# A four-turn expert loop: one turn more between row transposes and second products

## The chip, the cores and the metric

The kernel runs on one core of a Trainium2 chip. The metric is the device time of one execution in microseconds (us), the median of several runs. A core has a tensor engine (PE), a vector engine (DVE), a scalar engine (ACT), GpSimd (POOL) and a sync engine (SP). Each works through a list of its own in program order. They wait for each other by semaphores, and an engine that waits holds up all that stands behind the wait in its list. ACT and SP also issue plain transfers, POOL the indirect ones.

## The reference, cut to what matters

Two layers of cross attention, attention and feed forward run over 2048 tokens of 256 numbers. The last stage, the only one that the change touches, is a mixture of 160 experts with 8 chosen for each token:

```
h1     = silu(einsum('th,eih->eti', x, w_gate))      # first products
h1w    = h1 * combine.T[:, :, None]
routed = einsum('eti,ehi->th', h1w, w_down)          # second products
```

The kernel computes only the chosen pairs of token and expert, 16384 of them.

## The kernel before, in words

An earlier stage has sorted copies of the token rows into pages of 64 rows. All rows of a page have the same expert. There are 416 pages; eight of them are a unit, so there are 52 units, and a unit has two doubles of four pages. The function `experts` (line 938 on) works on them in a Python loop that is unrolled into the engines' lists. Its parts, for unit m:

- `load(m)`, SP: reads eight expert numbers from a table, waits until the second products of unit m-4 are done (`D.wait`, the ring of weights holds four units), and issues eight weight transfers of 256 KB (line 934). A number that is out of bounds makes the transfer skip itself: the page then uses weights that are there already.
- `rows_sp(m)`, SP: issues two of a unit's eight fetches of 64 rows (line 971). On SP the order is load(0), rows_sp(1), load(1), rows_sp(2) and so on, so `rows_sp(m+1)` stands behind `load(m)` and its wait.
- `rows_act(m)`, ACT: the other six fetches. `room_for` makes both wait until the results of unit m-8 are stored.
- `turn(m)`: eight PE transposes of rows (line 1001), then two DVE copies out of PSUM (line 1005).
- `up(m)`: 32 first products on PE (line 1016), which wait for the weights and for the copies of the turn; then one silu on ACT (line 1021).
- `flip(m)`: four PE transposes of the silu's result (line 1028), one DVE copy (line 1032).
- `down(m)`: sixteen second products (line 1042), two DVE copies to `y` (line 1048), and after each of them two indirect scatters by POOL into `y_d` (line 1052).
- `weigh(b)`: small DVE work on the routing weights (lines 1060 to 1073), four pieces in each turn of the loop.

A turn of the loop is, in PE's list, turn(m), down(m-2), flip(m-1), up(m). DVE's list has in one turn: two copies of turn(m), two copies of down(m-2), the copy of flip(m-1), weigh. PE's semaphores are counts: T for turn, U for up, V for flip, D for down. Such a signal is raised by the last matmul of its group.

After the loop a last stage reads all results back and sums eight for each token. It starts when the last scatter has landed.

Of the kernel before, what the change touches and what calls it, by code (L numbers as in the profile page):

```python
# [33 lines left out]
UNITS = DOUBLES // 2  # L34
# [903 lines left out]
def experts(nc, a, sem, bank, ident, table, xs_d, y_d, X, tops, rates, spots, wts, spare, rings, dchain, out):  # L938


    pe, dve, act, pool, sp = nc.tensor, nc.vector, nc.scalar, nc.gpsimd, nc.sync
    FLIP, DOWN, AHEAD, WEIGHED, EARLY = 1, 2, 4, 12, 3
    FETCHED, RESULTS, HELD = 16, 6, 2
    ex, pT, xw, slot_id, w, xgT, (hidden, h), s_rows, s_table, s_w = rings
    ph = ExitStack()
    with ph:
# [41 lines left out]
        def rows_act(m):  # L988
            page = load_numbers(nc, mybir.EngineType.Activation, table[1], m, 8)
            room_for(act, m)  # L990
            for k in range(at_sp(m), 8):
                fetch(act, m, k // 2, k % 2, page[k])

        def turn(m):
            pe.wait_ge(s_g[m % (FETCHED // 2)], (m // (FETCHED // 2) + 1) * 128)
            for d in (2 * m, 2 * m + 1):
                bk = bank[d % 2]
                T.wait(pe, "dve", d - 2)
                for c in range(2):
                    for g in range(2):  # L1000
                        last = pe.transpose(bk[:, (2 * c + g) * P:(2 * c + g + 1) * P], xg[:, d % FETCHED, g, c * P:(c + 1) * P], ident[:, :])  # L1001
                T.done("pe", last)
                T.wait(dve, "pe", d)
                U.wait(dve, "pe", m - HELD)
                T.done("dve", dve.tensor_copy(xgT[d % 4], bk[:, :]))  # L1005

        def up(m):
            bk = bank[2 + m % 2]
            pe.wait_ge(s_w[m % DEEP], (m // DEEP + 1) * 128)
            T.wait(pe, "dve", 2 * m + 1)  # L1010
            U.wait(pe, "act", m - 2)
            for g in range(4):
                for c in range(2):
                    for half in range(2):
                        at = (2 * c + g % 2) * P + half * PAGE
                        last = pe.matmul(bk[half * PAGE:(half + 1) * PAGE, g * P:(g + 1) * P], xgT[(2 * m + g // 2) % 4][:, at:at + PAGE],  # L1016
                                         w[m % DEEP * 8 + 2 * g + half][:, c * P:(c + 1) * P], start=(c == 0), stop=(c == 1))
            U.done("pe", last)
            U.wait(act, "pe", m)
            V.wait(act, "pe", m - HELD)  # L1020
            U.done("act", act.activation(hidden[m % HELD], bk[:, :], ACT.Silu))  # L1021

        def flip(m):
            bk = bank[4 + m % 2]
            U.wait(pe, "act", m)
            V.wait(pe, "dve", m - 2)
            for g in range(4):
                last = pe.transpose(bk[:, g * P:(g + 1) * P], hidden[m % HELD][:, g * P:(g + 1) * P], ident[:, :])  # L1028
            V.done("pe", last)
            V.wait(dve, "pe", m)  # L1030
            D.wait(dve, "pe", 2 * (m - HELD) + 1)
            V.done("dve", dve.tensor_copy(h[m % HELD], bk[:, :]))  # L1032
# [59 lines left out]
        for m in range(UNITS + DOWN):  # L1092
            if m < UNITS:
                turn(m)
            if DOWN <= m:
                down(m - DOWN)
            if FLIP <= m < UNITS + FLIP:
                flip(m - FLIP)
            if m < UNITS:
                up(m)  # L1100
                for n in range(min(2 * m + EARLY, m + AHEAD), min(2 * m + 2 + EARLY, m + 1 + AHEAD, UNITS)):
                    rows_act(n)
                for b in range(4 * m, 4 * m + 4):
                    weigh(b)
# [61 lines left out]
        for k in range(half_k + 1, TOPK):  # L1166
            m = k - half_k
# [643 lines left out]
def program(nc, a, out, plan):  # L1811
    ctx = ExitStack()
    with ctx:
# [7 lines left out]
        def sem(name):  # L1821
# [44 lines left out]
        phase2(nc, a, turns, keys_values, (tops, rates, spots, table, xs_d, xf_d), rings, sem, bank, X, XN, ident, small, dchain, pool_waits, resident,  # L1866
               kT, vv, *prepared[0:3], sc)
        experts(nc, a, sem, bank, ident, table, xs_d, y_d, X, tops, rates, spots, wts, spare, rings, dchain, out)


# [53 lines left out]
```

How the kernel before makes its waits and increments, by code:

```python
    def link(self, ins):  # L99
        self.n += 1
        ins.then_inc(self.sem, 1)
        self.eng.wait_ge(self.sem, self.n)
# [99 lines left out]
    def wait(self, eng, events, i):  # L202
        if i >= 0:
            e, k = max(self.at.get(event, ("pe", 1)) for event in ([events] if isinstance(events, str) else events))
            eng.wait_ge(self.sem[e], i * self.per[e] + k)
# [23 lines left out]
    def keys_values(i, banks_free=None):  # L229
        z = i % 2
        yield
        G.wait(sp, "v3", i - 2)
        sp.dma_start(cT[z][:, :, :], a["ctx2"][i]).then_inc(s_ctx[z], 16)
        yield
        pe.wait_ge(s_ctx[z], (i // 2 + 1) * 16)
        if i == 0:
            banks_free()
        for m in range(2):
# [34 lines left out]
def phase2(nc, a, turns, keys_values, routes, rings, sem, bank, X, XN, ident, small, dchain, pool_waits, resident, kT, vv, qs, qb, bg2, sc):  # L273
# [74 lines left out]
            pool.memset(xw[z][:, :, DIM:WIDE], 0.0).then_inc(s_set, 1)  # L348
        last_row = pool.to_reg(ROWS - 1)
        pe.transpose(bank[6][0:1, 0:P], sc[:, 7:8], ident[:, :]).then_inc(s_max, 1)
        dve.memset(ones_e[:, :], 1.0).then_inc(s_set, 1)
        dve.memset(lift[:, :], -1.0).then_inc(s_set, 1)
        dve.wait_ge(s_max, 1)
        dve.tensor_reduce(sc[0:1, 3:4], bank[6][0:1, 0:P], AX.X, ALU.max).then_inc(s_max, 1)
        pe.wait_ge(s_max, 2)
        pe.matmul(bank[7][:, 0:1], ones[0:1, 0, :], sc[0:1, 3:4], start=True, stop=True).then_inc(s_max, 1)
        dve.wait_ge(s_max, 3)
        link(dve.tensor_copy(sc[:, 2:3], bank[7][:, 0:1]))
```

## Time and profile before

| | us |
|---|---|
| median of 3 runs (1536.27 to 1544.11) | 1537.04 |
| span of the profiled execution | 1537.4 |
| the loop's steady part, 44 units | 365.56 |
| last scatters, 1461.91 to 1485.80 | 23.89 |
| last stage, 1485.80 to 1537.40 | 51.60 |

The profiled execution's span is 0.4 us above the median of the runs; nothing outside the span is reported. A start time in the rows below is counted from the start of the span. In the profile a matmul's end is modelled from its start, while the end of a copy or of a silu is measured.

### The profile page before, as it was taken

Reading aid. Unit: us, or ns where it says so; the run is one execution under the profiler, and the core shown is the slowest. Engines: PE = TensorE matmul, PEld = TensorE weight load, DVE = VectorE, ACT = ScalarE, POOL = GpSimd, SP = SyncE. Lnnn points to the kernel's source line nnn. Section 1 sums busy time; section 2 is a strip of 40 time slices with the busy share of each in tenths; the row PEclk is TensorE's granted clock in tenths of the full one; section 3 lists DMA queues with packets and bytes.
Section 4 is the critical chain, followed back from the end, with each engine's and each line's share of the span. In section 5 each row is a group of like instructions: output and inputs, shape, how many; then the busy total and the mean of one; then the engine's idle time right before and its main releaser. Section 6 shows DMA issues by size and latency. Waiting matters only on the chain. (4 is left out here: it accounts for less than half of the span.)

```text
span 1537.4 us, 34403 instructions
## 1 busy us (share of the span) xinstructions
PE 1310.5 (85%) x11693; PEld 947.1 (62%) x11693; DVE 934.3 (61%) x2676; ACT 595.3 (39%) x1709; POOL 549.3 (36%) x717
## 2 busy tenths in 40 slices
PE   5999999999986899999999998755777877787747
PEld 3676767667653676776667776634555555565525
DVE  2576667666654478777887777553544545454437
ACT  2455545454532666675666566310000000000031
POOL 0010111101001136666656564631445444454440
PEclk8999999999995899999999999987999999989968
DMA  9223424233220002111111211339565666665549
GB/s 305 85 72 120 142 75 144 96 121 120 73 95 28 15 23 68 62 51 60 67 58 52 77 35 41 96 108 291 149 180 165 165 192 180 188 186 172 152 159 366
DMA packets 124879, 185.73 MB, mean 121 GB/s; under 512 B 23286, under 2 KB 90517, under 8 KB 122785
## 3 DMA queue, kind: packets, MB, share of 16 engines
q1 hardware_dynamic: 53776, 91.55, 19.0%
q10 hardware_dynamic: 54800, 57.31, 12.4%
q0 software_dynamic: 16128, 34.67, 6.3%
q8 instruction: 95, 1.56, 0.4%
q14 instruction: 80, 0.65, 0.1%
HBM read 190.88 MB, written 78.25 MB: 175 GB/s over the span
## 5 line engine op out<-in xcount | busy, mean ns | idle before, releaser
L1052 POOL DMA_INDIRECT y_d<-y,xg x208 | 206.4, 992 | 258.9 <-DVE y L1048 211.1
L1005 DVE COPY ex<-bank 128x512 f32<-128x512 f32 x104 | 67.1, 686 | 230.1 <-issue 112.9
L1021 ACT ACTIVATE ex<-bank 128x512 f32<-128x512 f32 x52 | 31.0, 597 | 418.9 <-remote 224.8
L773 POOL DMA_INDIRECT xs_d<-xw,slot_id x128 | 135.0, 1055 | 29.8 <-issue 27.9
L472 ACT ACTIVATE ex<-bank,nmC 128x256 f32<-128x256 f32 x256 | 119.1, 483 | 13.1 <-DVE nmC L466 12.8
L485 PE MATMUL bank<-ident,ex 128*128 128x128 f32 x512 | 81.5, 290 | 19.1 <-ACT ex L472 16.9
L485 PEld LDWEIGHTS bank<-ident,ex 128*128 128x128 f32 x512 | 63.8, 149 | 54.1 <-ACT ex L472 21.3
L466 DVE TENSOR_REDUCE nmC<-bank 128x2 f32<-128x512 f32 x128 | 82.9, 682 | 5.7 <-PE bank L457 4.8
L1028 PE MATMUL bank<-ident,ex 128*128 128x128 f32 x208 | 35.8, 297 | 54.0 <-ACT ex L1021 52.1
L1311 POOL TENSOR_TENSOR stB<-stB,small 128x1 f32<-128x1 f32 x32 | 20.2, 632 | 165.3 <-DVE stB L1308 165.3
L1465 ACT ACTIVATE sm<-sm,nm 128x256 f32<-128x256 f32 x128 | 63.4, 499 | 36.0 <-DVE nm L1457 35.8
L491 ACT COPY pTC<-bank 128x512 f32<-128x512 f32 x112 | 64.9, 594 | 26.2 <-PE bank L485 19.1
L1685 POOL COPY recxB<-recB 128x128 f32<-128x128 f32 x32 | 8.4, 291 | 184.9 <-DVE recB L1680 184.9
L1028 PEld LDWEIGHTS bank<-ident,ex 128*128 128x128 f32 x208 | 22.7, 145 | 81.9 <-ACT ex L1021 78.6
L1048 DVE COPY y<-bank 128x512 f32<-128x512 f32 x104 | 66.9, 681 | 10.0 <-PE bank L1042 8.4
L1001 PE MATMUL bank<-ident,xg 128*128 128x128 f32 x416 | 61.0, 293 | 8.5 <-DMA xg<-xs_d 8.5
L1338 PE MATMUL bank<-cT,wk0a 128*128 128x512 f32 x128 | 63.8, 623 | 3.6 <-DVE nm L1457 3.6
L457 PE MATMUL bank<-kTC,qxC 32*128 32x256 f32 x512 | 61.1, 438 | 6.1 <-ACT ex L472 3.3
L1001 PEld LDWEIGHTS bank<-ident,xg 128*128 128x128 f32 x416 | 48.5, 150 | 19.5 <-issue 10.5
L1369 PE MATMUL bank<-pTA,ctxA 128*128 128x512 f32 x128 | 59.1, 605 | 0.7 <-DVE pTA L1485 0.4
L505 POOL TENSOR_TENSOR recx<-recC,half 128x128 f32<-128x128 f32 x64 | 24.1, 406 | 95.6 <-DVE recC L499 95.6
L472 ACT ACTIVATION_READ_ACCUMULATOR ex<-bank,nmC 128x1 f32 x256 | 54.8, 214 | 0.0
(390 smaller groups left out, 3418.2 us busy)
## 6 DMA issues: line engine op xcount, KB each, us to landing
xs_d<-zeros ACTq DMA_DIRECT2D x16, 1768.0 KB, 7.3
pTC<-in_wexp SPq DMA_DIRECT2D x104, 256.0 KB
xg<-xs_d ACTq DMA_DIRECT2D x306, 68.0 KB
cT<-in_ctx SPq DMA_DIRECT2D x32, 512.0 KB, 4.0
wh<-in_wexp SPq DMA_DIRECT2D x52, 256.0 KB
cT<-in_wexp SPq DMA_DIRECT2D x52, 256.0 KB
kTC<-in_wexp SPq DMA_DIRECT2D x52, 256.0 KB
vvC<-in_wexp SPq DMA_DIRECT2D x52, 256.0 KB
```

Source lines behind the costliest of these rows:

```text
L457: last = pe.matmul(bank[hp][:, 256 * b:256 * b + 256], qx[z][rows, m, b, :, :].rearrange("p h t -> p (h t)"), kT[z][rows, m, 256 * b:256 * ...
L466: D.done(i, "dve", dve.tensor_reduce(nm[:, u, :], bank[hp][:, :].rearrange("p (b n) -> p b n", b=2), AX.X, ALU.max, negate=True), f"m{u}")
L472: last = act.activation(ex[:, u, 256 * b:256 * b + 256], bank[hp][:, 256 * b:256 * b + 256], ACT.Exp, bias=nm[:, u, b:b + 1], accum_out=su ...
L485: last = pe.transpose(bk[:, q * P:(q + 1) * P], ex[:, u, q * P:(q + 1) * P], ident[:, :])
L491: D.done(i, en, copy(pT[:, u, :], bk[:, :]), f"pT{u}e")
L773: pool.indirect_dma_start(out=xs_d, out_offset=bass.IndirectOffsetOnAxis(ap=slot_id[z][:, k:k + 1], axis=0), in_=xw[z][:, k, :], in_offset ...
L1001: last = pe.transpose(bk[:, (2 * c + g) * P:(2 * c + g + 1) * P], xg[:, d % FETCHED, g, c * P:(c + 1) * P], ident[:, :])
L1005: T.done("dve", dve.tensor_copy(xgT[d % 4], bk[:, :]))
L1048: D.done("dve", dve.tensor_copy(y[:, n, :, :].rearrange("p g n -> p (g n)"), bk[:, :]))
L1052: pool.indirect_dma_start(out=y_d, out_offset=bass.IndirectOffsetOnAxis(ap=who, axis=0), in_=y[:, n, g, :], in_offset=None, bounds_check=l ...
L1338: pe.matmul(bank[m][:, :], wka[:, m * P:(m + 1) * P], cT[z][:, 0, :], start=True, stop=False)
L1465: last = act.activation(sm[:, j, n, :], sm[:, j, n, :], ACT.Exp, bias=nm[:, h:h + 1], scale=-1.0, accum_out=sums[:, h:h + 1])
```

## The change

The loop gets one more turn of depth. In turn m PE now does turn(m), up(m-1), flip(m-2), down(m-3); before it was turn(m), down(m-2), flip(m-1), up(m). The silu and the DVE copies move with their matmuls: DVE's list becomes two copies of turn(m), the copy of flip(m-2), two copies of down(m-3), weigh. The loop runs 55 turns and not 54. `rows_act` is called for unit m+3 and not m+4 in turn m. Since the silu in that turn is now that of unit m-1, the fetches of a unit keep their place behind the same silu. SP's list does not change, only the moment at which its waits on D are met. Rings, PSUM banks and the number of instructions stay as they are.

```diff
-    FLIP, DOWN, AHEAD, WEIGHED, EARLY = 1, 2, 4, 12, 3
+    UP, FLIP, DOWN, AHEAD, WEIGHED, EARLY = 1, 2, 3, 3, 12, 3
...
         for m in range(UNITS + DOWN):
             if m < UNITS:
                 turn(m)
+            if UP <= m < UNITS + UP:
+                up(m - UP)
+            if FLIP <= m < UNITS + FLIP:
+                flip(m - FLIP)
             if DOWN <= m:
                 down(m - DOWN)
-            if FLIP <= m < UNITS + FLIP:
-                flip(m - FLIP)
             if m < UNITS:
-                up(m)
                 for n in range(min(2 * m + EARLY, m + AHEAD), min(2 * m + 2 + EARLY, m + 1 + AHEAD, UNITS)):
                     rows_act(n)
```

## Rows read from the trace of the kernel before

**Rows 1.** Busy time by stage: loop's start, steady loop, last scatters, last stage
```profile
core 0: us, PE busy (x) PEld busy (x) DVE busy (x) ACT busy (x) POOL busy (x), PEclk, DMA share, GB/s
1033.00:1096.35 63.35, 38.80 (x365) 29.41 (x367) 23.92 (x63) 3.58 (x6) 15.87 (x16) 0.82 0.81 231
1096.35:1461.91 365.56, 288.26 (x2641) 211.55 (x2639) 177.68 (x465) 26.27 (x44) 174.83 (x176) 0.91 0.61 175
1461.91:1485.80 23.89, 14.26 (x122) 9.69 (x118) 7.55 (x12) 1.19 (x2) 15.66 (x16) 0.71 0.15 54
1485.80:1537.40 51.60, 29.75 (x100) 23.26 (x100) 34.18 (x85) 15.98 (x53) 0.00 (x0) 0.74 0.91 366
```
**Rows 2.** Timeline of PE, one period of the steady loop
```profile
1210.82 0.66 PE L1028 MATMUL bank<-ident,ex 128*128 128x128 f32 x4
1211.68 1.97 PE L1016 MATMUL bank<-pTC,ex 128*64 128x128 f32 x32 [0.20 <-issue]
1213.58 1.09 PE L1001 MATMUL bank<-ident,xg 128*128 128x128 f32 x8
1214.60 0.43 PE L1042 MATMUL bank<-kTC,ex 128*64 128x256 f32 x1
...
1217.02 0.42 PE L1042 MATMUL bank<-xw,ex 128*64 128x256 f32 x1 [0.36 <-issue]
1219.18 1.11 PE L1028 MATMUL bank<-ident,ex 128*128 128x128 f32 x4 [1.74 <-ACT ex L1021]
```
**Rows 3.** Timelines of ACT, POOL and DVE, the same period
```profile
1210.17 0.60 ACT L1021 ACTIVATE ex<-bank 128x512 f32<-128x512 f32 x1 [8.05 <-DMA y_d<-y,xg]
1218.53 0.60 ACT L1021 ACTIVATE ex<-bank 128x512 f32<-128x512 f32 x1 [7.76 <-remote]
...
1212.45 0.98 POOL L1052 DMA_INDIRECT y_d<-y,xg  x1 [3.71 <-DVE y L1048]
...
1216.30 0.98 POOL L1052 DMA_INDIRECT y_d<-y,xg  x1 [0.30 <-issue]
1220.75 0.98 POOL L1052 DMA_INDIRECT y_d<-y,xg  x1 [3.47 <-DVE y L1048]
...
1210.29 1.29 DVE L1005 COPY ex<-bank 128x512 f32<-128x512 f32 x2 [4.23 <-issue]
1211.49 1.28 DVE L1048 COPY y<-bank 128x512 f32<-128x512 f32 x2
1212.69 0.68 DVE L1032 COPY ex<-bank 128x512 f32<-128x512 f32 x1
1218.59 1.29 DVE L1005 COPY ex<-bank 128x512 f32<-128x512 f32 x2 [5.22 <-remote]
```
**Rows 4.** Timelines of PE, ACT and POOL: before the second group of scatters, and near the end
```profile
1066.92 1.27 PE L1016 MATMUL bank<-kTC,ex 128*64 128x128 f32 x9
...
1068.24 0.60 ACT L1021 ACTIVATE ex<-bank 128x512 f32<-128x512 f32 x1 [9.69 <-PE bank L1016]
...
1463.47 1.13 PE L1016 MATMUL bank<-kTC,ex 128*64 128x128 f32 x8
...
1464.64 0.60 ACT L1021 ACTIVATE ex<-bank 128x512 f32<-128x512 f32 x1 [5.75 <-PE bank L1016]
...
1461.91 0.98 POOL L1052 DMA_INDIRECT y_d<-y,xg  x1 [3.27 <-DVE y L1048]
...
1483.61 0.98 POOL L1052 DMA_INDIRECT y_d<-y,xg  x1 [0.30 <-issue]
```
**Rows 5.** Timeline of SP's transfers: first without scatters, then in rows 2's period
```profile
1065.04 2.98 SPq L934 DMA_DIRECT2D pTC<-in_wexp  x8
1068.53 1.13 SPq L971 DMA_DIRECT2D xg<-xs_d  x2
...
1211.88 1.21 SPq L971 DMA_DIRECT2D xg<-xs_d  x2
1213.82 0.26 SPq L934 DMA_DIRECT2D wf<-in_wexp  x1
1214.11 4.29 SPq L934 DMA_DIRECT2D cT<-in_wexp  x4
1218.52 0.61 SPq L934 DMA_DIRECT2D kTC<-in_wexp  x3
```
**Rows 6.** Chain of work through one unit's last scatter
```profile
1232.67 0.30 issue
1232.98 2.11 DMA y_d<-y,xg
```
**Rows 7.** DMA queues over 42 units: packets, MB, share of 16 engines
```profile
q1 hardware_dynamic: 19934, 29.94, 29.0%
```
**Rows 8.** Who waited for whom over the same 42 units: us, times, longest
```profile
PE bank L1028 <- ACT ex L1021: 48.4, 34, 2.6
```
**Rows 9.** Timeline of POOL, the loop's first scatter
```profile
1057.55 0.98 POOL L1052 DMA_INDIRECT y_d<-y,xg  x1 [38.24 <-DVE y L1048]
```

## The prediction

> **What bounds the kernel now.** I read the stretches by stage first [rows 1]. The loop's steady part has 176 scatters, so 44 units in 365.56 us: 8.31 us for a unit. PE is marked busy for 79% of it, POOL for 48%, DVE for 49%, and the DMA engines for 61%. No engine is full, so a loop of waits sets the period. I then laid the timelines of one period side by side to find it [rows 2, 3].
>
> PE's first products end at 1213.65 by their rows [rows 2], yet the silu that waits for nothing else starts at 1218.53 [rows 3], 4.9 us later. The transposes that follow them end at 1214.67, and their DVE copies start at 1218.59. So several PE signals of different ages arrive together. I call this moment the release. The preceding one is at 1210.17. PE being behind with its work does not explain it: thirty-two first products and the transposes behind them, which alone take 1.09 us [rows 2], can't end within 0.1 us of each other. Before the second group of scatters the first products end at 1068.19 and the silu starts at 1068.24. Near the loop's end, when SP issues no more weights, they end at 1464.60 and the silu starts at 1464.64, though POOL is scattering [rows 4].
>
> What stands beside the silent stretch is POOL's group of four scatters: it runs from 1212.45 to 1217.28, and the release follows 1.25 us behind [rows 3]. SP suffers in the same stretch: without scatters it issues eight weight transfers in 2.98 us; in the stretch four take 4.29 us [rows 5]. The first matmul group whose signal is lost ends 1.2 us after POOL's start (1213.65), and SP's slow stretch begins 1.66 us after it (1214.11). I read a closed loop: release, two copies of turn, the first copy of down, POOL's start, four scatters, release. In numbers [rows 3]: 1210.17 to 1212.45 is 2.28; POOL 4.83; then 1.25. That is 8.36 against the 8.31 of the mean. PE isn't on it: it needs some 5.5 us after the release and then stands still. This is the reading on which all below rests. It is inferred from times, and I know no cause for it.
>
> **What the change does to that loop.** No instruction is added or removed; the number of copies, scatters and transfers is the same. Four things move.
>
> First, the wait of flip for its silu goes. It cost PE 48.4 us in 42 units, 1.15 us each [rows 8]. PE isn't on the loop, so I count nothing; it is the cover for the half-speed stretches of PE (mean granted clock 0.91 [rows 1]). If PE were the bound it would be worth about 1.15 us a unit (a rival below).
>
> Second, DVE's order. Today three copies stand between release and POOL: two of turn, one of down. They start 0.60 us apart (1211.49 less 1210.29 is two of them [rows 3]). In the new list, turn(m) is the first thing PE does after a release, not the last before one. Its signals should be back before the silence, and its copies done while POOL scatters. The copy of flip now stands before that of down. Flip's matmuls come after the first products, some 3.9 us after the release, so their signal is caught in the silence. That leaves two copies between release and POOL: 2.28 − 0.60 = 1.68. The period is 1.68 + 4.83 + 1.25 = 7.76 us.
>
> Third, what may spoil it: the turn's rows arrive later. Load(m) waits for down(m-4). That used to come at the end of turn m-2, and now comes at the end of turn m-1, and rows_sp(m+1) stands behind it in SP's list while turn(m+1) needs it one period later. The slack was a period more. Count from a release: the queue moved 29.94 MB in 42 units [rows 7], of which 84 row fetches of 68 KB are 5.85, so 92 real weight transfers, 2.2 a unit. A skipped one takes 0.61 / 3 = 0.20 us of SP; the eight of 2.98 us, 0.37 each, I take as the price of a unit with more real ones than the mean [rows 5]. Eight of a mean unit then lie between 1.6 and 3.0 us, and I take 2.6. Add 0.3 for the wait and the first step, 0.5 for the table read between 1068.02 and 1068.53, and 1.13 for two fetches [rows 5]: 4.5 us if nothing disturbs. But the silence begins at 1.68 + 1.66 = 3.3 us. The weights fit, the table and the two fetches fall into it, at 4.29 / 4 = 1.07 us for a step or more; I let them end with it, at about 7.1 to 7.8. The landing isn't shown for them. Its nearest row is a scatter's, 2.11 us [rows 6]; below it I bound it by 0. So rows are there 7.1 to 9.9 us after the release, that is between 0.7 us before the next release and 2.1 us after it. The turn's second signal is raised about 1.4 us later (1.09 and 0.3), at 0.7 to 3.5 us of the next period. The silence takes signals from 1.68 + 1.2 = 2.9 us on. So most turns pass, the late ones are caught. A caught turn puts its two copies back in front of POOL: 2.28 + 0.60 = 2.88, a period of 8.96. If one turn in six is caught the mean is 7.76 + 0.2 = 7.96; that share is an estimate from where 2.9 lies between 0.7 and 3.5, reduced because most units have few real weights and a long period gives SP 1.2 us back. Bounds: none caught, 7.76; half caught, 8.36.
>
> Fourth, depth. The first scatter waits for one turn more, while the first turns are set by the arrival of weights and rows, as before. Every scatter is then a turn late at the start: +8.0 (7.8 at the new period, 8.3 at the old). At the end, from the 49th group's first scatter to the last scatter is 1483.61 + 0.98 − 1461.91 = 22.7 us [rows 4]; there the groups follow each other almost at once, and I count no change. The last stage of 51.60 [rows 1] keeps its work.
>
> **The Trainium skill against the rows.** The rows show SP's plain transfers at 1.07 us each beside POOL's scatters, and at 0.37 without them [rows 5]. The Trainium skill, page "DMA: Bandwidth & Descriptors", section "SWDGE vs HWDGE vs iDMA", says that GpSimd writes its descriptors into rings in SBUF by software and that transfers issued by SP or ACT never use that path. By that rule SP's fetches would be out 4.5 us after the release, no turn would be caught, and the sum would be that of 7.76. The trace does not agree: something is shared.
>
> A second rule gives a rival. In the rows the silu starts 4.9 us after the modelled end of the matmuls [rows 2, 3]. The Trainium skill, page "Perfetto Trace Analysis", section "Tensor Engine Instruction (MATMUL, LD_WEIGHTS)", says that PE's end in a profile is an estimate, and that the signal is sent when PSUM has acknowledged all bytes. By that a late signal would mean late matmuls, and PE would be the bound; the silu and the turn's copy 0.06 us apart speak against it.
>
> **The sum.** From the fourth group of scatters to the 49th there are 45 periods. 45 × (7.96 − 8.31) = −15.8, and +8.0 for depth: −7.8. Against the profiled span: 1537.4 − 7.8 = 1529.6. The span stands 0.4 above the median of the runs, so I say 1529.2. With the bounds of the period: 7.76 gives 1537.4 − 24.8 + 8 = 1520.6; 8.16, a third caught, gives 1538.7.
>
> **Rivals.** *The silence is thinner.* With SP waiting more for D, PE's signals may come back early, as in rows 4, or PE is truly the bound and wins the 1.15 us of its wait. Then the period is 8.31 − 1.15 = 7.16: 45 × −1.15 + 8 = −44, 1494. For it: the prompt silu of rows 4 [rows 4], and PE's late signals if they were late matmuls. Against: the bunch of signals [rows 3]. The skill's second rule above, if it held here, would be this rival. A milder form, flip's signal also ahead of the silence, gives 1.08 + 4.83 + 1.25 = 7.16 as well. Chance 0.15 for 1515 and less.
>
> *Turns are caught in half of the periods.* Mean 8.36: the copies that left the loop come back, and only depth is left: +2.3 + 8 = +10, 1548. For it: signals of the turn due at up to 3.5 us against 2.9. Against: 2.2 real weights a unit leave the mean unit earlier. Chance 0.25 for 1539 to 1552.
>
> *Slower by SP's chain.* If the wait for down(m-4), eight weights and two fetches together end later than 2.9 − 1.4 = 1.5 us after the next release, every turn, PE starts each turn late, second products slide past the release and POOL starts a further 0.5 us or more late: a period of 8.86 and above, 45 × 0.55 + 8 = +33, 1570. It decides when the landing takes over 2.5 us. For it: up(m) too has its weights only one period after load(m) may start. Against: they are issued in 2.6 us, ahead of the silence. Chance 0.15 for over 1552.
>
> The forecast keeps 0.45, for 1515 to 1539.
>
> **Numbers.** About 0.5% (7.7 us) is what a measurement of this kernel can tell from no change: below 1529.3 is faster, above 1544.7 slower. Of the forecast's 0.45, 0.27 lie below 1529.3. Faster is 0.27 + 0.15 = 0.42. Of the 0.25 for half caught 0.10 lie below 1544.7, so the same is 0.18 + 0.10 = 0.28; slower is 0.15 + 0.15 = 0.30. The range that leaves out 2 in 10 is 1507 to 1558; the forecast's own is 1515 to 1539.
>
> **What would show it.** In the profile after: POOL's groups 7.8 to 8.0 us apart; from silu's start to POOL's first scatter about 1.7 us; copies of line 1005 in POOL's shadow and not just behind the silu; SP's two fetches of line 971 between 3 and 8 us after the silu; PE without a wait for ACT on line 1028; the first scatter some 8 to 14 us later than 1057.55 [rows 9]. The prediction is wrong if four copies stand ahead of POOL in most periods, if POOL's groups come closer than 7.5 us, or if PE waits for rows or weights by more than 1 us a turn.

## The result, and the profile after

The changed kernel takes 1552.18 us (4 runs, 1550.0 to 1554.29), the kernel before on the same chip 1537.67 (4 runs). The ratio is 1.0101, 95% interval 1.0078 to 1.0124: slower by 1.0%, 14.5 us. The forecast was 1529.2, faster. The profiled execution has a span of 1553.0 us against 1537.4 before.

First the busy time by stage, cut as in [rows 1]: loop's start, steady loop from the fourth group of scatters to the 49th, last scatters, last stage.

```profile
core 0: us, PE busy (x) PEld busy (x) DVE busy (x) ACT busy (x) POOL busy (x), PEclk, DMA share, GB/s
1033.00:1103.99 70.99, 46.41 (x392) 35.59 (x392) 28.21 (x75) 4.18 (x7) 15.75 (x17) 0.79 0.74 209
1103.99:1476.82 372.83, 278.06 (x2646) 208.16 (x2648) 188.03 (x456) 26.30 (x44) 173.21 (x176) 0.93 0.59 171
1476.82:1500.00 23.18, 8.54 (x86) 5.71 (x82) 5.93 (x9) 0.60 (x1) 15.68 (x16) 0.78 0.16 55
1500.00:1553.00 53.00, 29.03 (x100) 22.79 (x100) 34.18 (x85) 15.99 (x53) 0.00 (x0) 0.77 0.88 357
```

The steady 44 units take 372.83 us, 8.47 each, where they took 8.31. PE is busy for less of it. The moments come from POOL's timeline: first scatter, fourth group, 49th group, last scatter.

```profile
1069.64 0.99 POOL L1052 DMA_INDIRECT y_d<-y,xg  x1 [49.67 <-DVE y L1048]
...
1095.14 0.98 POOL L1052 DMA_INDIRECT y_d<-y,xg  x1 [2.87 <-DVE y L1048]
...
1476.82 0.98 POOL L1052 DMA_INDIRECT y_d<-y,xg  x1 [4.11 <-DVE y L1048]
...
1497.60 0.98 POOL L1052 DMA_INDIRECT y_d<-y,xg  x1 [0.30 <-issue]
```

The first scatter is 12.1 us later than in [rows 9], the fourth group 7.0 us (1088.18 before). The 45 periods between take 381.68 us, 8.48 each; before 8.305. That is +8.0 us. The rest gives +0.7: the tail is 0.9 shorter, the work behind the last scatter 1.6 longer. 7.0 + 8.0 + 0.7 = 15.6, which is the difference of the spans.

Now who waited for whom on PE in the steady loop (total us, times, longest), against [rows 8]:

```profile
PE bank L1001 <- DMA xg<-xs_d: 70.9, 38, 3.6
PE bank L1042 <- issue: 17.3, 37, 1.1
```

Flip's wait for ACT is gone, as the change intended. In its place the transposes wait for their rows, 70.9 us in all, 1.6 us a unit. Two periods show how; SP and PE first, then POOL, ACT and DVE. (The transposes at 1226.49 are of rows that were there in time.)

```profile
1226.68 0.08 SPq L934 DMA_DIRECT2D wf<-in_wexp  x1
1226.94 2.70 SPq L934 DMA_DIRECT2D cT<-in_wexp  x4
1231.07 1.66 SPq L934 DMA_DIRECT2D kTC<-in_wexp  x3
1233.35 1.14 SPq L971 DMA_DIRECT2D xg<-xs_d  x2
...
1226.49 1.09 PE L1001 MATMUL bank<-ident,xg 128*128 128x128 f32 x8
...
1236.34 1.09 PE L1001 MATMUL bank<-ident,xg 128*128 128x128 f32 x8 [2.29 <-DMA xg<-xs_d]
...
1241.47 1.95 PE L1042 MATMUL bank<-pTC,ex 128*64 128x256 f32 x16
```

```profile
1226.65 0.98 POOL L1052 DMA_INDIRECT y_d<-y,xg  x1 [5.16 <-DVE y L1048]
...
1230.56 0.98 POOL L1052 DMA_INDIRECT y_d<-y,xg  x1 [0.30 <-issue]
1234.39 0.98 POOL L1052 DMA_INDIRECT y_d<-y,xg  x1 [2.85 <-DVE y L1048]
...
1243.57 0.98 POOL L1052 DMA_INDIRECT y_d<-y,xg  x1 [4.34 <-DVE y L1048]
...
1232.76 0.60 ACT L1021 ACTIVATE ex<-bank 128x512 f32<-128x512 f32 x1 [8.08 <-remote]
...
1228.89 1.29 DVE L1005 COPY ex<-bank 128x512 f32<-128x512 f32 x2
1232.82 0.69 DVE L1032 COPY ex<-bank 128x512 f32<-128x512 f32 x1 [2.64 <-remote]
```

A group of second products ends at about 1226.5. SP, which waited for it, issues eight weights until 1232.7 and two fetches of rows from 1233.35 to 1234.49. The transposes that need them start at 1236.34, 9.8 us behind the second products. First products, flip and second products follow in PE's list and end at 1243.4. That end is what SP waits for next but one: from one second product to that of two turns later it is 16.9 us, two periods of 8.45. This is a closed chain: neither the transposes nor SP's next weights can come earlier than it allows.

The first period shown, 1226.65 to 1234.39, is 7.74 us, the next 9.18. Of the 45, 24 are under 8.1 us and have a mean of 7.78, the other 21 have 9.29. In the short ones the loop runs as forecast: POOL ends at 1231.54, the silu starts 1.22 us later, and POOL starts 1.63 us behind the silu, with the copies of the turn (1228.89) in its shadow. Over all 24 the median from the silu to POOL's start is 1.70 us.

The profile shows one thing more. SP itself waits little for the second products:

```profile
SPq L934 <- PE bank L1042: 11.3, 12, 2.1
```

Between these waits its list takes 8.26 us a unit (mean over units 5 to 46, reading of the tables included), of a period of 8.5. In the kernel before it takes 8.30 us of 8.33 on this chip and is idle ahead of one load in 42. There no engine waited for it, since the rows arrived 8.1 us ahead of their transposes (mean); now PE waits for what comes out of this full list. So the chain through the second products and SP's list by itself are nearly of one length here, and this chip's profile can't part them.

### The profile page after: what moved, and what is told of

It reads as the page before. It is cut to its first block and busy times, and to the rows that moved or that the text cites. A ratio compares the mean times of both kernels' runs of the same rounds, so it can differ in the third digit from the quotient of the medians.

```text
span 1553.0 us, 34403 instructions
## 1 busy us (share of the span) xinstructions
PE 1303.3 (84%) x11693; PEld 947.4 (61%) x11693; DVE 946.3 (61%) x2676; ACT 595.8 (38%) x1709; POOL 548.4 (35%) x717
## 5 line engine op out<-in xcount | busy, mean ns | idle before, releaser
L1001 PE MATMUL bank<-ident,xg 128*128 128x128 f32 x416 | 66.6, 311 | 104.5 <-DMA xg<-xs_d 98.6
L1001 PEld LDWEIGHTS bank<-ident,xg 128*128 128x128 f32 x416 | 51.7, 156 | 127.3 <-DMA xg<-xs_d 119.3
L1032 DVE COPY ex<-bank 128x512 f32<-128x512 f32 x52 | 36.0, 692 | 150.8 <-PE bank L1028 103.3
L1005 DVE COPY ex<-bank 128x512 f32<-128x512 f32 x104 | 68.2, 687 | 68.2 <-issue 36.9
L485 PE MATMUL bank<-ident,ex 128*128 128x128 f32 x512 | 82.1, 292 | 19.4 <-ACT ex L472 17.5
L485 PEld LDWEIGHTS bank<-ident,ex 128*128 128x128 f32 x512 | 64.3, 150 | 54.2 <-ACT ex L472 22.0
L1048 DVE COPY y<-bank 128x512 f32<-128x512 f32 x104 | 71.4, 690 | 17.8 <-PE bank L1042 14.3
L457 PEld LDWEIGHTS bank<-kTC,qxC 32*128 32x128 f32 x512 | 36.3, 203 | 26.0 <-ACT ex L472 13.4
```

The source lines that it names most:

```text
L457: last = pe.matmul(bank[hp][:, 256 * b:256 * b + 256], qx[z][rows, m, b, :, :].rearrange("p h t -> p (h t)"), kT[z][rows, m, 256 * b:256 * ...
L485: last = pe.transpose(bk[:, q * P:(q + 1) * P], ex[:, u, q * P:(q + 1) * P], ident[:, :])
L1048: D.done("dve", dve.tensor_copy(y[:, n, :, :].rearrange("p g n -> p (g n)"), bk[:, :]))
```

## The experiments

They ran on five chips, each ratio against the kernel before on the same chip. The first chip has no number in the record, so that of e13 and e14, where the kernel before takes 1536.10, may be the same one. Each run is the kernel before or the changed one but for the edit shown.

### The change on other chips

No edit. e5 and e12 are the changed kernel, e6 the kernel before for its trace.

> The changed kernel itself, on whatever chip this call gets. In the first set the kernel before took 1379 and not 1537 us, with no late PE signals; the period there was 5.5 us. Theory A (SP's chain from down(m-4) through eight loads and two fetches to turn(m+1), two periods long): without late signals the chain is about 0.2 + 4.6 + 1.5 + 2 = 8.3 us to turn(m+1) plus 4.9 us from turn to the signal of down, 13.2 / 2 = 6.6 us a period, 1537's counterpart plus 50 us: 1425 to 1440 us where the kernel before takes 1379, PE waiting for rows. Theory C (the loss is depth alone): plus 6 to 9 us, 1386 to 1390. On a chip like the first, A: 1552, C: 1545.

> The kernel before itself, for its trace on this chip. If the late PE signals belong to the chip and not to the kernel, the silu starts either 0.3 us (period 5.4 to 5.6) or 4.6 us (period 8.3) behind the first products in nearly all units, and the same holds for e5.

> The changed kernel itself once more, as the measure for the other three on their chip. If the kernel before takes about 1379 there: 1475 to 1500, period 7.3 to 7.7, ratio 1.07 to 1.085 as before. If it takes about 1537: 1548 to 1556, ratio 1.008 to 1.012, period 8.4 to 8.5.

The kernel before takes 1378.78 us on the chip of e5 and e6, 1379.92 on that of e12: 10% less than on the first chip. The changed kernel takes 1486.53 (ratio 1.0776, 1.0730 to 1.0822) and 1486.21 (1.0786, 1.0751 to 1.0821). My 6.6 us for e5 was too short; it has 7.55 us a period, e12 7.38. What differs for the kernel before is seen in e6's timeline of ACT:

```profile
1204.59 0.60 ACT L1021 ACTIVATE ex<-bank 128x512 f32<-128x512 f32 x1 [4.64 <-PE bank L1016]
1209.95 0.60 ACT L1021 ACTIVATE ex<-bank 128x512 f32<-128x512 f32 x1 [4.76 <-PE bank L1016]
```

Silus are 5.4 us apart. Over all units the silu starts 0.38 us (median) after the start of the last first product, on the first chip 4.61 us. The late signals on which the prediction rests are all but absent here (over 1 us in 5 of 52 units, in 49 on the first chip), and PE sets the period. Busy time from the fourth to the 49th group, e6:

```profile
1056.80:1304.10 247.30, 244.40 (x2706) 184.10 (x2704) 189.20 (x470) 26.88 (x45) 178.60 (x181) 0.99 0.90 262
```

PE is busy for 99% of it. In the changed kernel the same chain is in the open. SP's and PE's timeline in e12, behind it the sums of PE's waits for rows and of SP's for second products, and the busy time of the 45 periods:

```profile
1178.31 0.08 SPq L934 DMA_DIRECT2D wf<-in_wexp  x1
1178.58 1.86 SPq L934 DMA_DIRECT2D cT<-in_wexp  x4
1180.62 0.61 SPq L934 DMA_DIRECT2D kTC<-in_wexp  x3
1181.86 1.14 SPq L971 DMA_DIRECT2D xg<-xs_d  x2
...
1187.25 1.09 PE L1001 MATMUL bank<-ident,xg 128*128 128x128 f32 x8 [3.73 <-DMA xg<-xs_d]
```

```profile
PE bank L1001 <- DMA xg<-xs_d: 70.8, 26, 6.8
...
SPq L934 <- PE bank L1042: 90.5, 31, 8.2
...
1070.90:1403.20 332.30, 261.40 (x2706) 198.70 (x2708) 193.33 (x470) 26.88 (x45) 176.96 (x180) 0.93 0.67 194
```

Here SP's list takes 5.34 us of the period of 7.4, so it is not full, and both waits of the chain can be seen. Against e6 the 45 periods are 85.0 us longer. PE idles for 68.0 of these. The other 17.0 are the same matmuls running longer: after the waits PE's granted clock is in part at the lower level, 0.93 in the mean where e6 has 0.99.

Taken over units 5 to 46, the chain's parts are (means, us):

| | first chip, after | e12 |
|---|---|---|
| second products to SP's first weight | 0.6 | 0.3 |
| eight weights | 5.6 | 2.5 |
| to the first fetch | 0.8 | 0.8 |
| first fetch to the rows' arrival | 2.9 | 4.4 |
| arrival to the transposes | 0.3 | 1.0 |
| transposes to the end of second products | 6.9 | 5.9 |
| sum, two turns | 17.0 | 14.9 |

17.0 / 2 = 8.5 and 14.9 / 2 = 7.4. That these are the measured periods proves nothing by itself, since the parts lie end to end from one unit's second products to those of two units later. What shows the chain at work is how little slack its two waits leave: SP starts 0.6 and 0.3 us behind the second products, where it lagged by 3.6 in the kernel before on the first chip, and the transposes start 0.3 and 1.0 us behind their rows' arrival, where it was 8.1 us. And it shows in what follows when the chain is cut, below. On the first chip that stands against 8.3 us which the late signals took already; elsewhere against PE's 5.4. So the same chain costs 1% there and 8% here.

### Taking the chain apart

e7 and e8 (and again e15, e16): changed kernel and kernel before without weight transfers from unit 4 on, and so without SP's wait for D; the first and second products use the weights of the first four units.

```diff
-            load(m)
+            if m < DEEP:
+                load(m)
...
-            pe.wait_ge(s_w[m % DEEP], (m // DEEP + 1) * 128)
+            pe.wait_ge(s_w[m % DEEP], 128)
```

> The changed kernel with only the first four units' weights loaded and no wait for down(m-4) on SP: units 4 to 51 use what lies in the ring. Theory A: SP no longer hangs on second products, no wait for rows or weights, PE's work sets the period, 5.2 to 5.4 us on a chip without late signals; level with e8 but for depth, within 8 us of it, and 20 us or more below the kernel before. Theory B (the order itself): the loss against e8 stays at over 2%.

> The kernel before with the same weights left out. Theory A: weights land in time before, so only the waits near the loop's start go: 0 to 20 us faster than the kernel before, period as before. If transfers of weights were what slowed the rest (bandwidth), the period would fall clearly.

> The changed kernel without weight transfers and without SP's wait for them from unit 4 on, a second time, in the hope of a chip on which the kernel before takes 1537 (late PE signals); it took 1384 where before took 1379. On a chip of 1537: the release loop on which the prediction rests gives a period of 7.76 (two copies between the release and POOL's start) and about 1520; if the late signals need weight transfers beside the scatters they are gone and it is 5.4 and about 1400. On a chip of 1379: 1384 again.

> The kernel before, without weight transfers from unit 4 on, a second time. On a chip of 1537: if POOL's scatters alone hold back PE's signals the period stays at 8.3 and the time at 1530 to 1537; if weight transfers are needed for it the period is 5.4 to 6 and the time about 1400. On a chip of 1379: 1375 again.

e7 takes 1383.95 (1.0037, 1.0019 to 1.0055), e8 1374.91 (0.9980, 0.9963 to 0.9997). Both have a period of 5.40. On another chip e15 gives 1383.15 (1.0038, 1.0023 to 1.0053) and e16 1376.88 (0.9984, 0.9964 to 1.0003). Without the chain, then, the change costs the difference, 9.0 and 6.3 us: the turn of depth, for which I had 8.0. (The fourth group is 9.4 and 6.8 us later, with a turn of 5.4 us.) The other 100 us or so of e5's and e12's loss come from SP's weights and its wait for D ahead of them. Both chips take 1379 for the kernel before, so e15 and e16 did not test the late signals.

e10: SP waits for D in every unit, but issues no weights from unit 4 on (the products use the first four units' weights).

```diff
             D.wait(sp, "pe", 2 * (m - DEEP) + 1)
-            load_weights(nc, a, which, m, w, s_w)
+            if m < DEEP:
+                load_weights(nc, a, which, m, w, s_w)
```

> The changed kernel in which SP still reads the table and still waits for down(m-4) in every unit, but from unit 4 on issues no weight transfers; the first products use the weights of the first four units, so that the output is another one. It stands between the changed kernel (wait and transfers) and the run without both (1383.95). Theory, the chain is long because the rows queue behind eight weight transfers: without these the rows leave within 1.5 us of the second products and land about 2 us later, 3.5 to 4 us, less than a turn of 5.4: no waits of the transposes in the steady part, period 5.40 to 5.45, 1382 to 1388. Rival, the wait on SP alone costs: the transposes wait for rows in every second turn, period 6 or more, over 1410.

1384.08 (1.0026, 1.0013 to 1.0040), period 5.44, as expected. Its transposes (one line further down in its kernel, 1002) waited for rows twice in 45 periods:

```profile
PE bank L1002 <- DMA xg<-xs_d: 1.5, 2, 1.4
```

The wait alone is free, since the rows are there 4.5 us behind the second products (medians: first fetch after 0.7, arrival 3.8 later) and a turn has 5.4. The eight weights in front of them make it 8 in e12, on the same chip. The Trainium skill, page "DMA: Bandwidth & Descriptors", section "Queues, rings and completion order", says that SP has one ring on each DMA engine and that descriptors are consumed in ring order. By that the rows would also queue behind the weights' bytes. The runs bear out little of it: 4.4 us with weights ahead, 3.8 without. What delays the rows is mostly that SP issues them 3 us later.

e1: changed kernel, SP fetches the rows of unit m+2, not m+1, behind load(m), from unit 4 on. e2: the same edit in the kernel before, as a control. e11: changed kernel, from the fourth unit on ACT fetches all rows.

```diff
             load(m)
-            if m + 1 < UNITS:
-                rows_sp(m + 1)
+            for n in ([m + 1] if m < EARLY else [m + 1, m + 2] if m == EARLY else [m + 2]):
+                if n < UNITS:
+                    rows_sp(n)
...
-            return 4 if m < EARLY else AT_SP
+            return 4 if m < EARLY else 0
...
-            if m + 1 < UNITS:
+            if m + 1 < EARLY:
                 rows_sp(m + 1)
```

The first part is the edit of e1 and e2, the rest that of e11.

> The changed kernel, with SP's two row fetches taken out of the new chain: from unit 4 on they are issued one unit earlier, rows_sp(m+2) behind load(m) and not rows_sp(m+1). Theory A (SP's chain: signal of down(m-4), eight loads, two fetches, landing, turn(m+1), ..., down(m-2) is two periods long and sets them at 8.48 us): PE's wait for rows of 161 us goes, the release loop of 7.76 us is left, 45 periods win about 30 us, 1515 to 1530 us, below the kernel before. Theory B (the new order of PE and DVE is itself slow, second products end late whatever the rows do): the wait moves to another place, period 8.3 to 8.5, 1545 to 1555 us.

> The kernel before with the same earlier row fetches. There the rows land 6 to 10 us before their turn, so theory A expects no change: period 8.3 us, 1534 to 1541 us. If the fetches' place in SP's list matters by itself (they collide less with the scatters, theory B'), it is faster by over 8 us.

> The changed kernel with all eight row fetches of a unit issued by ACT from the fourth unit on, so that no row stands behind weights in SP's list. Theory: the waits of the transposes vanish as they did when SP fetched rows a unit earlier (1411.85, ratio 1.022); the first products' wait for weights, 23.5 us there, stays, since load(m) still has little more than a turn. Period 5.8 to 6.0, 1400 to 1412, ratio 1.015 to 1.024. Rival: the rows are late because the whole chip's transfers are (16 DMA engines busy with weights), whoever issues them: waits on L1001 of over 1 us a turn and a period above 6.5. A second rival: two more issues a unit delay ACT's silu, seen as waits of the second transposes for ACT.

The first four runs (e1 to e4) were written down for a kernel before of about 1537 us; their chip had it at 1379.28, so only direction and waits can be held against the text. e1 takes 1411.85 (1.0223, 1.0191 to 1.0256), e2 1378.74 (0.9993, 0.9973 to 1.0014), e11 1424.98 (1.0327, 1.0303 to 1.0351). PE's waits in the steady part, e1 and then e11:

```profile
PE bank L1016 <- DMA pTC<-in_wexp: 14.6, 7, 3.3
PE bank L1016 <- DMA kTC<-in_wexp: 6.1, 5, 2.8
```

```profile
PE bank L1001 <- DMA xg<-xs_d: 19.1, 20, 2.5
PE bank L1028 <- ACT ex L1021: 17.9, 19, 2.0
```

Rows a turn earlier take away the wait of the transposes and 70% of the loss (32.6 us where e5 has 107.8); then the first products wait for weights, over 20 us, since load(m) still has little more than a turn. The kernel before has slack for both, so e2 changes nothing. e11 was expected at 1400 to 1412 and costs more than e1: its second rival came true, eight fetches in ACT's list delay the silu, and flip waits for ACT again.

### The order within a turn

e4: kernel before with DOWN = 3 and nothing else. e3 and e18: kernel before with down(m-2) ahead of turn(m). The first two lines of the diff are e4, the rest is e3. e9 makes the same move in the changed kernel, with down(m-3) first; in e14 it stands second.

```diff
-    FLIP, DOWN, AHEAD, WEIGHED, EARLY = 1, 2, 4, 12, 3
+    FLIP, DOWN, AHEAD, WEIGHED, EARLY = 1, 3, 4, 12, 3
...
+            if DOWN <= m:
+                down(m - DOWN)
             if m < UNITS:
                 turn(m)
-            if DOWN <= m:
-                down(m - DOWN)
```

> The kernel before with second products one turn later alone: DOWN = 3, up and flip stay in their places (AHEAD = 4 stays). Theory A: the signal of down(m-4) comes one period later, so SP's chain binds as in the changed kernel; PE waits for rows, period 8.4 to 8.8, and with one turn of depth 1550 to 1565 us. Theory B (the move of up and flip is what costs): period 8.3 as before, depth alone, 1540 to 1547 us.

> The kernel before with down(m-2) ahead of turn(m), in PE's list and in DVE's. It tests the release loop. If the two turn copies between release and first scatter are on the loop, the first scatter follows the release by 2.28 - 1.20 = 1.08 us, the period is 7.2 us and the time 1537 - 45 x 1.1 = about 1488 us. If PE or SP is the bound (60 matmuls or SP's list take 8.3 us whatever DVE does), the period stays 8.1 to 8.4 us and the time 1530 to 1542 us.

> The kernel before with down(m-2) ahead of turn(m), a second time. On a chip of 1537 it tests the release loop: only the first copy of down then stands between the release and POOL's start, 0.9 to 1.1 us where 2.28 were, so the period is 7.0 to 7.2 and the time 1478 to 1490. If there is no such loop, it costs PE the wait for the turn's copies as on the chip of 1379 (+0.9%): 1545 to 1555. On a chip of 1379: 1393 again.

> The changed kernel with one call moved: in each turn down(m-3) stands first, ahead of turn(m), up(m-1), flip(m-2), where it stood last. Depth, copies and transfers are unchanged; what moves is the moment at which down(m-4)'s signal lets SP load weights, from the end of turn m-1 to its start, nearly one turn (5 us) earlier. Theory, the two-turn chain through SP (second products, weights, rows behind them, next transposes): its 8 to 9 us from second products to the rows now have two turns less one group of second products, about 9 to 11 us, so the waits of the transposes in the steady part nearly vanish. Period 5.4 to 5.6 us where the kernel before has 5.5, time 1384 to 1395 beside a kernel before of 1379, ratio 1.003 to 1.012. Rival, the transfers share bandwidth and are late wherever the wait stands: the waits for rows or weights stay above 1 us a turn, period 6.5 or more, time over 1430. On a chip where the kernel before takes 1537, the chain adds nothing more either: within 1% of it.

> The changed kernel, four turns deep, with down(m-3) in second place: turn(m), down(m-3), up(m-1), flip(m-2). With down first, each unit's second products stood directly behind its flip and waited 0.87 us for the copy; now a turn's transposes lie between. Down(m-4) ends 2.7 us into turn m-1, some 2.7 us sooner than in the changed kernel. Theory, the chain through SP: it takes 8 to 9 us and now has 10.8 - 2.7 = 8.1 to turn(m+1): short waits of the transposes for rows, 0 to 0.9 a unit, period 5.45 to 5.9, and depth: 1385 to 1408, ratio 1.004 to 1.021. Rival: the chain is not what binds in the changed kernel, but its order of first products ahead of second ones, or depth itself: period over 6.5, over 1430.

e4 takes 1417.89 (1.0263, 1.0228 to 1.0299). Its waits:

```profile
PE bank L1016 <- DMA pTC<-in_wexp: 11.6, 7, 2.7
PE bank L1016 <- DMA kTC<-in_wexp: 10.1, 6, 3.8
PE bank L1001 <- DMA xg<-xs_d: 3.2, 3, 2.2
```

Second products one turn later are by themselves enough to make SP's transfers late, in the old order of the rest. It is the weights that PE waits for here, though, and hardly the rows, on which I had put it: down(m-3) stands second in PE's list, so SP starts sooner than in the changed kernel. e3 takes 1393.35 (1.0089, 1.0063 to 1.0115) and e18 1393.02 (1.0103, 1.0086 to 1.0120), both on chips of 1379: first products so close behind the transposes wait about 0.6 us in each unit, by the order of the lists for the copies (25.9 us in 44 waits, which the profile calls "issue"). The release loop, which e18 was to test, could not be tried there.

e9 takes 1415.68 (1.0266, 1.0243 to 1.0288), where I expected 1384 to 1395. Its waits:

```profile
PE bank L1042 <- DVE ex L1032: 34.9, 44, 1.2
```

The part on the chain was right: no transposes wait in the steady part; rows arrive 7.95 us behind the second products, as in e12, and lie 4.4 us before they are used. But I had overlooked that down(m-3) at the start of a turn stands directly behind flip of the same unit at the end of the last one, and waits 0.8 us for its copy: period 6.25.

e14 puts a turn's transposes between. On the chip where the kernel before takes 1536.10 it takes 1560.47 to 1587.45 (ratio 1.0200, 1.0156 to 1.0244). I had written for a chip of 1379, so the time can't be held against the text, but the run is a miss for the account: second products that come sooner should have shortened the chain, and e14 loses 2.0% where the changed kernel lost 1.0% on the first chip. Its profiled execution is one of its longest (1584.71). In it the transposes wait for rows for 12.5 us only, and second products for DVE's copy of flip for 96.8 us in 32 waits. So the wait for rows went and another took its place; whether the shorter executions have it too is not known.

e13: each turn runs turn(m), flip(m-2), up(m-1), down(m-2). The unit is spread over three turns as before; flip's silu has cover, and down's place as seen from SP is that of the kernel before, but for the length of a turn's first part.

```diff
-    UP, FLIP, DOWN, AHEAD, WEIGHED, EARLY = 1, 2, 3, 3, 12, 3
+    UP, FLIP, DOWN, AHEAD, WEIGHED, EARLY = 1, 2, 2, 4, 12, 3
...
             if m < UNITS:
                 turn(m)
-            if UP <= m < UNITS + UP:
-                up(m - UP)
             if FLIP <= m < UNITS + FLIP:
                 flip(m - FLIP)
+            if UP <= m < UNITS + UP:
+                up(m - UP)
             if DOWN <= m:
                 down(m - DOWN)
```

> Depth and the lost cover taken apart: the unit is spread over three turns as before, but each turn runs turn(m), flip(m-2), up(m-1), down(m-2). Flip's silu has a turn's second products and transposes as cover, and down's copy has the first products between. Down(m-4), for which SP waits before load(m), ends at the end of turn m-2, where it ended in the kernel before; up(m) comes one turn later than there. So the rows have two turns (10.8 us) for the 8 to 9 that the chain takes, and the weights more than two. Theory: no wait on L1001, L1016, L1028 or L1042 in the steady part, period 5.40 to 5.45 (the floor of both kernels without weights), no turn of depth added; the first scatter some 2 us later than before (first products ahead of second ones). Against before 45 x -0.08 = -3.6 and +2: 1374 to 1382, ratio 0.996 to 1.002. Rival, a unit that has its first products a turn later costs whatever down's place is: period over 5.8, over 1395. On a chip where the kernel before takes 1537: flip's copy and flip's wait no longer stand between the silu and POOL, 1510 to 1540.

On the chip where the kernel before takes 1536.10 it takes 1504.33 (0.9810, 0.9776 to 0.9844), 32 us less and better than the 1510 to 1540 expected. No other edit beats the kernel before by more than 0.2%. Busy time of its steady part, the one wait for rows in it, and a period of POOL, ACT, DVE and PE:

```profile
1083.20:1425.60 342.40, 274.57 (x2709) 204.80 (x2708) 188.83 (x470) 26.88 (x45) 177.48 (x181) 0.97 0.65 189
```

```profile
PE bank L1001 <- DMA xg<-xs_d: 0.7, 1, 0.7
```

```profile
1204.54 0.98 POOL L1052 DMA_INDIRECT y_d<-y,xg  x1 [2.81 <-DVE y L1048]
...
1208.44 0.98 POOL L1052 DMA_INDIRECT y_d<-y,xg  x1 [0.30 <-issue]
1212.25 0.98 POOL L1052 DMA_INDIRECT y_d<-y,xg  x1 [2.82 <-DVE y L1048]
...
1203.22 0.60 ACT L1021 ACTIVATE ex<-bank 128x512 f32<-128x512 f32 x1 [6.89 <-remote]
1210.76 0.60 ACT L1021 ACTIVATE ex<-bank 128x512 f32<-128x512 f32 x1 [6.94 <-remote]
...
1203.57 0.69 DVE L1048 COPY y<-bank 128x512 f32<-128x512 f32 x1 [4.30 <-PE bank L1042]
...
1206.78 1.29 DVE L1005 COPY ex<-bank 128x512 f32<-128x512 f32 x2
1207.98 0.68 DVE L1032 COPY ex<-bank 128x512 f32<-128x512 f32 x1
...
1204.33 1.09 PE L1001 MATMUL bank<-ident,xg 128*128 128x128 f32 x8
...
1205.26 0.60 PE L1028 MATMUL bank<-ident,ex 128*128 128x128 f32 x4
```

The period is 7.61 us. From the silu to POOL's start it is 1.32 us where the kernel before has 2.28 on the first chip [rows 3], because only the copy of down stands between; POOL's group takes 4.88 and the silu follows 1.34 behind it. That the gain comes from the copies is argued from these rows and not separated from two other things: flip's wait for ACT is gone as well, and SP's list, which is full here too, takes 7.63 us of the period and not 8.30. There is no profile of the kernel before on this chip, and e13 was not run on a chip of 1379.

### The late signals

e17: kernel before, POOL writes the results by plain transfers to rows in order, so that they land in other rows.

```diff
-                    pool.indirect_dma_start(out=y_d, out_offset=bass.IndirectOffsetOnAxis(ap=who, axis=0), in_=y[:, n, g, :],
-                                            in_offset=None, bounds_check=last_pair, oob_is_err=False).then_inc(s_y[n], 16)
+                    at = (2 * d + g) * P
+                    pool.dma_start(y_d[at:at + P, :], y[:, n, g, :]).then_inc(s_y[n], 16)
```

> The kernel before, in which POOL writes each result block with a plain transfer to rows of its own in place of the indirect scatter (the rows land in another order, so that the output is another one). On a chip of 1537: if the indirect scatters hold back PE's signals, the silu follows the first products by 0.3 to 0.5 us in all units and the period falls to 5.4 to 6, about 1400 or less; if not, the signals stay 3 to 5 us late and the time within 3% of 1537. On a chip of 1379: POOL's group shrinks, period stays at PE's 5.4 to 5.5, 1365 to 1380.

Its chip had the kernel before at 1379.88; it takes 1378.23 (0.9992, 0.9974 to 1.0011). POOL's plain write is 0.54 us where a scatter is 0.98, and it changes nothing there. It says nothing of a chip of 1537.

## Why the prediction was wrong

**What bounds the kernel now.** The release loop was read on one chip. On the four chips of 1379 us it isn't there. Where the kernel before takes 1537 its outline holds: the silus that are over 1 us late start, in the median, 1.12 us behind POOL's end in the kernel before (49 units of 52), 1.24 in the changed one (32), 1.40 in e13 (49). The time from such a silu to POOL's start falls with the copies between them: 2.28 us with three, 1.70 with two, 1.31 with one (e13). And the short periods of the changed kernel have 7.78 us against the forecast's 7.76, though these 24 were picked for being short. In e13 DVE's copies of turn and flip start while POOL scatters, at 1206.78 and 1207.98. That doesn't speak against the silence: their transposes end, as modelled, at 1205.42 and 1205.86, before or just at the moment from which the prediction has signals caught (1204.54 + 1.2). Why the silu's signal comes only when POOL is done is not known. What the reading left out is SP's own list, full in the kernel before as well, 8.30 us of 8.33. Whether SP's list fills the period or sets it no run tells.

**First, flip's wait counted as nothing.** It went (50.9 us before over these 45 periods), and the period did not fall. No run takes it away alone on such a chip, so its price stays open.

**Second, DVE's order.** Right in mechanism and size where the rows are in time: 1.70 us from silu to POOL where I had 1.68.

**Third, the later rows: the step that failed.** "If one turn in six is caught the mean is 7.96." Instead 21 of 45 periods were long, with a mean of 9.29, and hardly because the turn's signals were caught (the turn's copies start while POOL scatters, as forecast, in 42 of 52 units): PE stood waiting for rows, by 1.6 us a turn, over the 1 us that the prediction itself named as a sign of being wrong. The end of the row's way was near: 9.85 us behind the second products, against 7.1 to 9.9. That is in part luck. Eight weights took 5.6 us and not 2.6, since it was they that fell beside the scatters, and the fetches, on which I had put that delay, took 1.1. Landing took 2.9 against 0 to 2.11.

What was wrong is what I measured it from. I counted from the release, as if it came each 7.76 us whatever the rows did, and asked only whether the turn's signal would still pass. But turn(m+1) stands first in PE's list, so late rows shift first products, flip and second products too, and SP's next wait hangs on these: 9.85 + 0.3 + 6.9 = 17.0 us for two turns. The chain should have been closed and halved: 8.5. Even so my numbers would not have given it. For the last term I had 5.5 us (PE's work after a release), and (9.9 + 0.3 + 5.5) / 2 is 7.85. The 6.9 is measured: in the second period shown PE runs at a mean granted clock of 0.76 behind its wait, and in the first its second products take 4 us beside the scatters (1230.00 to 1234.05) where they take 1.95 at 1241.47.

Nor did I add up SP's list. By my own numbers it was 7.3 to 8.0 us a unit (fetches end at 7.1 to 7.8, less 0.3 at the start, and 0.5 for the next table), as long as the period it was held against; it measured 8.26. The account comes nearest to the rival "slower by SP's chain", which I gave 0.15, at a smaller price than its 8.86: the delay is shared by two turns.

**Fourth, depth.** +8.0 forecast. +7.0 at the fourth group on the first chip, where the loop also began 1.8 us earlier than before, and 9.0 and 6.3 us as the whole difference where the chain is taken out (e7 less e8, e15 less e16).

**The sum.** From 7.96 to 8.48 a period, 45 times, is +23.5 us, which is what separates 1529.6 from the 1553.0 of the profiled span; the other terms are off by less than 2 us. The time of 1552.2 lies in the range of 1507 to 1558, but the change is the other way than the forecast.

**The two rules that the prediction cites.** The first, in the Trainium skill, page "DMA: Bandwidth & Descriptors", section "SWDGE vs HWDGE vs iDMA", tells by which path descriptors go; I had drawn from it that SP's issue would not be slowed beside scatters. On the first chip it is: eight weights take 5.6 us in the changed kernel and 2.5 in e12, the same program. On the chip of e12 the row at 1178.58, four weights in 1.86 us, stands beside scatters that run from 1178.29, and the trace agrees with what I drew. The second, in the Trainium skill, page "Perfetto Trace Analysis", section "Tensor Engine Instruction (MATMUL, LD_WEIGHTS)", says that PE's ends are estimates. On the chips of 1379 the silu follows the start of the last matmul by 0.3 to 0.4 us, where the model gives that matmul 0.27, so the estimate is close there; whether PE is truly late where the kernel before takes 1537 stays open.

Still open: what makes the signals late where the kernel before takes 1537, and whether the release loop or SP's full list sets the period there. e15 to e18 were meant to tell, and came to a chip of 1379. The chain through SP is shown by experiments on chips of 1379 only (e7, e10, e1); for the first chip it is read from the profile.

## What to carry to other kernels

Before a stage is deepened to hide one wait, follow the semaphores by which its buffers are given back, and close the chain over as many turns as it spans: last reader, loads, what is queued behind the loads, first reader, last reader again. Its sum over its turns is a floor of the period, and moving the last reader to a turn's end lengthens it. Add up, too, how long each engine's own list takes for one turn, the engines that only issue transfers included: none of these sums may exceed the period that is forecast. On one chip a wait was hidden at the old depth by changing the order within a turn (e13). A bound that was read on one chip should be looked for on a second before an edit is priced by it.

## What the runs showed of the hardware

The same kernel, with the same instructions, takes 1379 to 1380 us on four chips, and 1537 on the first and 1536 on that of e13, which may be the first again. Between the profiles of the first chip and of e6 there are 160 us. Of these 126 lie in the 45 periods of the loop (8.3 against 5.5 us a unit), 23.5 ahead of the loop's first weight transfer. In the loop the difference goes with silus that start 4.6 us after the start of the last first product and not 0.4 (medians); in the changed kernel on the first chip it is 2.0 and in e13 3.2. PE's granted clock in that part of the kernel before was 0.91 of full speed on the first chip, so in part at the lower of its two levels (1.2 GHz), and 0.99 on the chip of e6. SP's eight weight issues with the steps between take 5.6 us on the first chip and 2.5 in e12. With no weights ahead of them the rows' fetches take 3.8 us to arrive (e10); I had bounded a landing by a scatter's 2.11.
